# A four-layer transformer on one core: attention and output projection on pairs of fp16 instead of pairs of fp32r

## The reference

```python
q = _rmsnorm(x @ wq_a.T, q_a_ln_w) @ wq_b.T            # 32 heads x (64 nope + 64 rope)
ckv, k_pe = split(x @ wkv_a.T)                          # 64 + 64, shared by all heads
kv = _rmsnorm(ckv, kv_a_ln_w) @ wkv_b.T                 # per head: 64 of k_nope, 128 of v
q_pe, k_pe = rope(q_pe), rope(k_pe)
scores = (q_full @ k_full.T) * softmax_scale            # causal, 512 x 512 per head and batch
out = softmax(scores) @ v
x = x + out.reshape(B, S, 4096) @ wo.T
```

## Time and profile before

| what | us |
| --- | --- |
| device time, median of 3 runs | 1870.42 |
| the runs | 1863.43 to 1874.71 |
| the profiled execution, its own time | 1868.27 |
| its span | 1866.4 |
| `first` (to 172.0) | 172.0 |
| `lora_layer0` (to 441.0) | 269.0 |
| `projections` (to 533.7) | 92.7 |
| `attention` (to 1240.0) | 706.3 |
| `out_projection` (to 1602.0) | 362.0 |
| `lora_layer1` (to 1866.4) | 264.4 |

### The profile page before, as it was taken

The page is one execution under the profiler, slowest core; times in us unless marked ns, Lnnn a source line. Parts: engine busy times, 40 slices in busy tenths (PEclk is TensorE's granted clock), DMA queues, the critical chain, the costliest instruction groups (busy, mean ns, idle before and its releaser), DMA issues. The chain is left out here.

```text
span 1866.4 us, 32180 instructions
## 1 busy us (share of the span) xinstructions
PE 1716.2 (92%) x12720; PEld 1318.2 (71%) x12720; DVE 1045.2 (56%) x2405; ACT 889.3 (48%) x1600; POOL 753.7 (40%) x601
## 2 busy tenths in 40 slices
PE   6896699997789999999999999969999999589998
PEld 5564355554468888888888888857888888345654
DVE  6697465655766666666666666644324322244343
ACT  5553411103657877877877877843213111231110
POOL 3222244445647666675766675620000000134441
PEclk8798799998989999999999999979999999789999
DMA  9673423234418877978878877888445221332322
GB/s 328 215 250 123 130 57 91 68 91 107 87 35 141 164 160 142 165 145 162 148 161 143 162 150 145 151 205 277 136 137 190 91 96 63 103 85 68 91 68 79
DMA packets 514437, 252.39 MB, mean 135 GB/s; under 512 B 437104, under 2 KB 487280, under 8 KB 513904
## 3 DMA queue, kind: packets, MB, share of 16 engines
q1 hardware_dynamic: 514288, 250.34, 56.0%
HBM read 97.21 MB, written 44.04 MB: 76 GB/s over the span
## 5 line engine op out<-in xcount | busy, mean ns | idle before, releaser
L1568 POOL TENSOR_TENSOR xb<-xb 128x1280 f16<-128x1280 f32 x128 | 337.9, 2640 | 8.3 <-ACT xb L1462 8.3
L1505 DVE TENSOR_REDUCE D_sv<-D_S 128x1 f32<-128x512 f32 (+2 forms) x384 | 234.9, 640 | 114.9 <-PE D_S L1403 114.9
L48 PE MATMUL F_o<-F_wh,N_hT 128*128 128x384 f16 (+1 forms) x768 | 258.1, 336 | 6.5 <-DVE F_wl L780 6.5
L49 PE MATMUL F_o<-F_wl,N_hT 128*128 128x384 f16 (+1 forms) x768 | 257.9, 336 | 0.0
L50 PE MATMUL F_o<-F_wh,N_hT 128*128 128x384 f16 (+1 forms) x768 | 257.4, 335 | 0.0
L1454 ACT ACTIVATE xb<-D_S,D_sv 128x512 f32<-128x512 f32 (+3 forms) x512 | 241.8, 526 | 26.3 <-DVE D_sv L1505 26.1
L92 POOL TENSOR_SCALAR mv<-mv 128x1 f32<-128x1 f32 x64 | 27.2, 426 | 560.5 <-DVE mv L87 559.5
L48 PE MATMUL E_o<-E_mh,E_oh 128*128 128x512 f32 x512 | 200.5, 392 | 10.3 <-DVE E_ol L1734 10.3
L50 PE MATMUL E_o<-E_mh,E_ol 128*128 128x512 f32 x512 | 200.1, 391 | 0.0
L49 PE MATMUL E_o<-E_ml,E_oh 128*128 128x512 f32 x512 | 200.1, 391 | 0.0
L1574 POOL TENSOR_TENSOR D_qs<-D_qs,D_t 128x256 f32<-128x256 f32 x128 | 93.9, 734 | 234.5 <-DVE D_t L1531 234.5
(11 more groups left out here) (203 smaller groups left out, 3968.5 us busy)
## 6 DMA issues: line engine op xcount, KB each, us to landing
E_ro<-otd SPq DMA_DIRECT2D x58, 512.0 KB, 4.5
A_wo<-in_wo SPq DMA_DIRECT2D x16, 1024.0 KB, 6.0
otd<-h SPq DMA_DIRECT2D x64, 256.0 KB, 2.8
mwd<-A_mst SPq DMA_DIRECT2D x32, 256.0 KB, 2.4
xd<-xb SPq DMA_DIRECT2D x16, 512.0 KB, 3.5
E_rm<-mwd SPq DMA_DIRECT2D x16, 512.0 KB, 4.5
xb<-xd SPq DMA_DIRECT2D x16, 512.0 KB, 6.1
out_x<-xb SPq DMA_DIRECT2D x16, 512.0 KB, 3.1
```

Source lines behind the costliest of these rows:

```text
L48: e.matmul(out, a[0], b[0], start=start, stop=False, **kw)
L49: e.matmul(out, a[0], b[1], start=False, stop=False, **kw)
L1505: e.tensor_reduce(s[:, part:part + len(tiles)], Sb[n % 4][:, 0:N].rearrange("p (i k) -> p i k", i=len(tiles)), AX.X, ALU.min).then_inc(s_n ...
L1568: e.tensor_tensor(P2[u % 3][:, 1280:2560], P[u % 3][:, :], P2[u % 3][:, 0:1280], ALU.subtract).then_inc(s_pl, 1)
```

## The change

All that the latent attention and the output projection multiply is kept as fp16 pairs.

- **Scales.** The absorbed query weights are weighted with both norm vectors, given one scale for each head group, and split in the first adapter layer (`QueryWeights`, tiles 5 to 12 for the eight groups, results in `wbs`). Each group costs there two loads, four products on DVE (`dve_weigh`), a sum of squares (ACT), a matmul with ones (PE, a turn "s"), a scale (POOL), the inverse (DVE), the high part (ACT, 1024 elements for each partition) and the low part (DVE, the same), and a store. `wa`'s split moves from tile 6 to tile 3. The scale of M comes from sums of squares that ACT takes in `first` behind each evacuation of M (`msq`).
- **Projections.** No pointer scale at the split of q and k; POOL's `split_wb` is gone; group 0's weights are loaded ready.
- **Attention.** Scores use the exact tile widths (512, 384, 256, 128). The exponentials have the group's negative inverse scale as a pointer beside the bias, and the bias is the minimum times the inverse, which DVE computes in `bias(u, 0)` (behind `least(u, 1)`) and `bias(u, 1)` (behind `low_q(u+2)`). `least(u, 2)` is two reductions. PE's `turn_o` and ACT's `out_o` are replaced by `high_o` (ACT, 256 elements, every unit) and `low_o` (POOL, every unit); the outputs of four units are stored as an fp16 pair to `od`, not turned. Values and turned queries have a bank each.
- **Output projection.** M is split once, 1024 columns wide, with its scale; the split of the outputs is gone, since SP loads them with a transposing DMA into `OT` (three buffers; by quarters for the first three tiles, whole tiles of 32 blocks later). Both halves of a tile are computed in one pass; the sums are scaled back as they are added (two adds for a tile, pointer scale). M's first load waits for all stores of `attention`.
- **Second adapter layer.** The load of `mean` moves ahead of the last weight loads.

```diff
+    def dve_weigh(self, e, w, g, vec, lnr, wa):
+        u = self.u[g % 2]
...
+        for k in range(2):
+            un = u[:, k, 0:256].rearrange("p (h r) -> p h r", h=4)
+            e.scalar_tensor_tensor(un, un, vec[:, k:k + 1], lnr[:, :].unsqueeze(1).to_broadcast([128, 4, 64]), ALU.mult, ALU.mult)
+            i = e.tensor_scalar(u[:, k, 256:512], u[:, k, 256:512], vec[:, k:k + 1], wa.col(wa.INV), ALU.mult, ALU.mult)
+        i.then_inc(self.s_u, 1)
+    def act_square(self, e, w, g, junk):
+        w.wait_ge(self.s_u, g + 1)
+        e.activation(junk, self.u[g % 2], ACT.Square, accum_out=self.col(self.SQ, g)).then_inc(self.s_sq, 1)
+    def act_high(self, e, w, g):
...
+        e.activation(self.hl[g % 2][:, 0, :, :], self.u[g % 2], ACT.Copy, scale=self.col(self.SCALE, g)).then_inc(self.s_hi, 1)
+    def dve_low(self, e, w, g):
...
+        e.scalar_tensor_tensor(self.hl[g % 2][:, 1, :, :], self.u[g % 2], self.col(self.SCALE, g), self.hl[g % 2][:, 0, :, :],
+                               ALU.mult, ALU.subtract).then_inc(self.s_lo, 1)
...
# first, ACT
-                e.activation(mst[n % 4][:, :], mb[hf][:, :], ACT.Copy, scale=vec[:, 2:3]).then_inc(s_me, 1)
+                e.activation(mst[n % 4][:, :], mb[hf][:, :], ACT.Copy, scale=vec[:, 2:3]).then_inc(s_mc, 1)
+                e.activation(mb[hf][:, :], mb[hf][:, :], ACT.Square, scale=vec[:, 2:3],
+                             accum_out=msq[:, 2 * kt + hf:2 * kt + hf + 1]).then_inc(s_me, 1)
...
# lora_layer0
-    WA = 6
+    WA, QW, MS = 3, 5, 13
...
         if t == WA:
-            ORDER += [("s", 4)]
+            ORDER += [("s", 4), ("s", MS)]
+        if QW <= t < QW + 8:
+            ORDER += [("s", 5 + t - QW)]
...
# lora_layer0, DVE, loop over tiles
+            if QW <= t < QW + 8:
+                qw.dve_weigh(e, w, t - QW, vec, lnr, wa)
             gate(t)
             low_w(t)
+            if QW < t <= QW + 8:
+                qw.dve_inverses(e, w, t - QW - 1)
+                qw.dve_low(e, w, t - QW - 1)
             finish(t)
             adapter(t)
...
# attention
-                    M = max(128 * (i + 1), 256)
+                    M = 128 * (i + 1)
...
-                m = e.activation(p[:, AT[i]:AT[i] + N], Sb[n % 4][:, c:c + N], ACT.Exp, scale=-1.0, bias=s[:, 3 - i:4 - i])
+                m = e.activation(p[:, AT[i]:AT[i] + N], Sb[n % 4][:, c:c + N], ACT.Exp, scale=qw.col(qw.NEG, g), bias=s[:, 7 - i:8 - i])
...
+        def high_o(u):
+            g, b, h = units[u]
+            o = os[u // 4 % 2]
+            w.wait_ge(s_o, u + 1)
+            w.wait_ge(s_ot[u // 4 % 2], 16 * (u // 8))
+            e.activation(o[:, :, 0, 64 * h:64 * h + 64], on[u % 2][:, :, :], ACT.Copy).then_inc(s_oh, 1)
...
-            if pair(u - LAG - 1):
-                out_o(u - LAG - 1)
+            if there(u - LAG - 1):
+                high_o(u - LAG - 1)
...
+        def bias(u, n):
+            g, s = units[u][0], sv[u % 4]
+            w.wait_ge(s_neg, 3 * u + 2 + n)
+            e.tensor_scalar(s[:, 4 + 2 * n:6 + 2 * n], s[:, 2 * n:2 * n + 2], qw.col(qw.INV, g), None, ALU.mult).then_inc(s_bias, 1)
...
                 least(u, 0)
                 least(u, 1)
+                bias(u, 0)
...
             if there(u + 2):
                 low_q(u + 2)
+            if there(u):
+                bias(u, 1)
...
+        def low_o(u):
...
+            e.tensor_tensor(o[:, :, 1, 64 * h:64 * h + 64], on[u % 2][:, :, :], o[:, :, 0, 64 * h:64 * h + 64], ALU.subtract).then_inc(s_ol, 1)
...
# out_projection
+        for kt in range(16):
+            for j in range(G):
+                product(j, kt)
+        for j in range(G, NT):
+            for kt in range(16):
+                product(j, kt)
...
+                e.scalar_tensor_tensor(dst, ob[2 * (j % 3) + hf][:, :], ms.col(ms.INV), dst, ALU.mult, ALU.add).then_inc(s_add, 1)
...
+        for i in range(2):
+            w.wait_ge(s_ot[i], 16 * 16)
         load_m(0)
...
+        for j in range(G, NT):
+            w.wait_ge(s_col, j - 2)
+            e.dma_start_transpose(OT[j % 3][:, :, :, :, :].rearrange("p g l k c -> p (g l k) c"),
+                                  od[j, :, :, :, :].rearrange("p g l c -> p (g l c)")).then_inc(s_o[j % 3], 16)
...
# lora_layer1, SP
+        e.dma_start(mean[:, :], a["cst"][:, C_MEAN:C_N]).then_inc(lw.s_bias, 16)
```

More of the change, by code:

```diff
@@ new lines, with __init__, sem, col @@
+class FusedScale:
+    def __init__(self, nc, root, msq):
+        def sem(what):
+            return root.enter_context(nc.semaphore(f"ms_{what}"))
+        self.msq = msq
+        self.c = root.enter_context(nc.sbuf_tensor("ms_c", [128, 4], F))
+        self.s_sum, self.s_red, self.s_sc, self.s_inv = sem("sum"), sem("red"), sem("sc"), sem("inv")
+    def col(self, i):
+        return self.c[:, i:i + 1]
+    RAW, TOTAL, SCALE, INV = 0, 1, 2, 3
+    def pe_total(self, e, w, ones, bank):
+        e.matmul(bank[:, 0:32], ones[:, :], self.msq[:, :], start=True, stop=True).then_inc(self.s_sum, 1)
+    def dve_total(self, e, w, bank):
+        w.wait_ge(self.s_sum, 1)
+        e.tensor_reduce(self.col(self.RAW), bank[:, 0:32], AX.X, ALU.add).then_inc(self.s_red, 1)
+        w.wait_ge(self.s_red, 1)
+        return e.tensor_scalar(self.col(self.TOTAL), self.col(self.RAW), NORM2, 1e-30, ALU.mult, ALU.max)
+    def pool_scale(self, e, half):
+        e.tensor_tensor(self.col(self.SCALE), self.col(self.TOTAL), half, ALU.pow).then_inc(self.s_sc, 1)
+    def dve_inverse(self, e, w):
+        w.wait_ge(self.s_sc, 1)
+        e.reciprocal(self.col(self.INV), self.col(self.SCALE)).then_inc(self.s_inv, 1)
@@ L1079, in pool @@
                 scale(4)
+                scale(MS)
+            if QW <= t < QW + 8:
+                scale(5 + t - QW)
         norm.pool_rstd(e, w, N_F0 + NT + 3)
@@ L1421, in values @@
             m.then_inc(s_v, 1)
-        def turn_o(u):
-            ps, o = t_bank("o", u), os[u // 2 % 2]
-            w.wait_ge(s_o, u + 1)
-            bank_empty("o", u)
-            for i in range(4):
-                m = e.matmul(ps[:, 128 * i:128 * i + 128], o[:, i, :], ident, start=True, stop=True, is_transpose=True)
-            m.then_inc(s_to, 1)
         for u in range(FIRST, LAST):
@@ L1574, in add_q @@
             e.tensor_tensor(qv[:, :, 64:128], qv[:, :, 64:128], m[:, :, :], ALU.add).then_inc(s_qr, 1)
-        for u in range(FIRST, NU + 1):
+        def low_o(u):
+            g, b, h = units[u]
+            o = os[u // 4 % 2]
+            w.wait_ge(s_oh, u + 1)
+            e.tensor_tensor(o[:, :, 1, 64 * h:64 * h + 64], on[u % 2][:, :, :], o[:, :, 0, 64 * h:64 * h + 64], ALU.subtract).then_inc(s_ol, 1)
+        for u in range(FIRST, LAST):
             if there(u + AQ - 1):
-                g, b, tt = units[u + AQ - 1]
                 add_q(u + AQ - 1)
-                if g + 1 < 8 and b == 2 and tt in (0, 2):
-                    split_w(g + 1, tt // 2)
             if there(u - 1):
                 low_p(u - 1)
+            if there(u - LAG - 1):
+                low_o(u - LAG - 1)
     def sp(e):
@@ L1610, in sp @@
                 load_w(units[u + AQ][0] + 1)
-            if pair(u - LAG - 1):
-                store_o(u - LAG - 1)
+            if there(u - LAG - 2) and (u - LAG - 2) % 4 == 3:
+                store_o(u - LAG - 2)
     with nc.Block() as block:
@@ L1775, in dve @@
+        for kt in range(16):
+            low_m(kt)
+        for j in range(NT):
+            add(j)
+            if j == 3:
+                w.wait_ge(s_add, 2)
                 norm.dve_stats(e, w, N_F1, xb[:, 0, :])
```

471 lines of the change are left out of this document (197 added, 274 removed).

## The result

The changed kernel took 1891.59 us (median; 1889.33 to 1898.38), the kernel before 1866.93 us over all its runs beside it (1861.27 to 1874.71). The ratio is 1.0135 (95% interval 1.0086 to 1.0185): slower by 1.35%. The forecast was 1898 us. The profiled execution has a span of 1888.1 us, 21.7 more than before's.

What follows compares the result with a forecast made beforehand. PE was taken to bound the attention and output projection before, a closed ACT-DVE loop the attention after. Attention +17, projection -6, first adapter layer +16, first attention +2.5, rest -0.3 and +1: 1868.3 + 30 = 1898 us; range 1845 to 1930.

Steps and rivals of the forecast that it cites:

- The attention's sum: Latent attention: units of 5.47 us instead of 5.31, +17 us; +20.9 with the start of the output projection.
- the ACT loop: Latent attention: closed chain over ACT and DVE through exponentials, `high_q`, `low_q` and bias, forecast at 5.47 us per unit.
- The price of the exponentials' pointers: Latent attention: a scale pointer costs each exponential 0.09 us, making the pairs 1.34 and 0.91 us.
- the rival built on it: Latent attention: pointers and bias cost nothing in the loop, 5.1 us per unit, 1851 us in all; chance 0.14.
- So the turn is one closed loop, and its length is a sum: Latent attention: `exps(u,2)` waits for the bias, behind `low_q`, which waits for `high_q`; steps add to 5.42 us per unit.
- The rule of the Trainium skill: Latent attention: an SBUF-to-SBUF `tensor_scalar` can fully block against POOL; priced at some 0.05 us per unit, 6 us.
- The rival in which PE sets the pace: Latent attention: the loop does not close and PE's 4.6 us per unit decide, 1791 us in all; chance 0.07.
- The rival in which the bias waits for `low_o` as well: Latent attention: `bias(u,1)` also waits for POOL's `low_o`, +100 us, 1998 us in all; chance 0.08.
- Output projection: Faster fp16 matmuls -17 us, PE's wait for tile 3 4.9, slower matmuls after it 1.5; with startup and last add -6.
- Start of the output projection: M's load waits for the last store, so the first matmul comes 11.5 us after it, not 7.6: +3.9 us.
- First adapter layer: Splitting query weights delays a0 and turn "s": five tiles +1.5 us, two with `wa`'s split +3.3; +16 in all.
- First attention: 32 squares of M on ACT, 0.68 us each, nearly all in idle time: +2.5 us.

Runs made afterwards that it cites:

- e1: Changed kernel with a constant scale instead of the pointer in the exponentials, subtraction of the maximum left out: 1887.7 us, ratio 1.0115.
- e5: Changed kernel with both the constant exponential scale of e1 and the one-element bias instructions of e2: 1854.9 us, ratio 0.9951.
- e2: Changed kernel with each two-element bias instruction made two instructions of one element: 1897.2 us, ratio 1.0166.
- e3: Changed kernel with `bias(u,1)` ahead of `low_q(u+2)` instead of behind it: 1963.3 us, ratio 1.0521.
- e4: Changed kernel with `bias(u,1)` ahead of `low_q(u+2)` and each bias as two one-element instructions: 1799.7 us, ratio 0.9639.
- e8: e4 with the queries computed seven units ahead instead of six: 1768.9 us, ratio 0.9493.
- e6: Changed kernel with DVE's inverse and low part of the query weights behind the tile's own work in the first adapter layer: 1914.2 us, ratio 1.0278.
- e9: e6 with the weighing of the query weights also moved, behind the gates: 1891.5 us, ratio 1.0144.
- e11: Changed kernel with PE's turn "s" behind the next tile's first chunk, DVE's total and POOL's scale following it: 1889.0 us, ratio 1.0126.
- e7: Changed kernel with M's first load issued ahead of the wait for the stores and four buffers for turned outputs: 1885.1 us, ratio 1.0120.

## Why the prediction was right, and what in it was not

The time was right to 6 us (the forecast increase was 30 us, the span grew by 21.7) and the sign for a true reason: a chain through several engines, which fp16 does not shorten, closes at 5.45 us and not at PE's 4.5. Of its steps:

- **The attention's sum** came out at +21.8 for +20.9 by errors that cancel. The 127 periods are 16.2 us longer, for 17 with the short turns at the ends. From the last unit's first score matmul to the issue of the last store it is 24.1 us for 19.3 before, +4.7 that no term had, less 0.9 at the stage's start. In the last stretch the biases of the last two units took 2.54 us each beside `low_p`, and ACT idled 1.2 us for each (0.5 before); how much of the 4.7 us they make is not shown. The start of the projection is +1.8 for +3.9. None of the signs that the prediction named (the gap behind `high_q`, a unit over 5.2 us) could tell the two loops apart: all came, and the ACT loop did not set the pace.
- **The price of the exponentials' pointers** (0.09 each): right, 1.32 and 0.91 measured for 1.34 and 0.91, and 0.36 us in e1 for the four. But the rival built on it, 5.1 us without them, is refuted as a mechanism in this order: e1 took them away and the time stood still.
- **"So the turn is one closed loop, and its length is a sum"**: the loop is there (e5) and its length was right (the forecast's 5.42 without the meeting with POOL, 5.42 by e2, as an estimate). It does not set the pace. The step that failed is the next one, where POOL was put inside the loop with room to spare and its meeting with the bias was priced at "I take 0.05". The meeting is itself a loop: bias, two minima, `bias(u,0)`, rotate, `add_q`, `low_p`, bias, 5.446 us. It costs only some 0.03 us per unit over the ACT loop in after, so the period came out right by luck, the two loops being that close; but the waiting instruction is what any repair of ACT runs into: 0.36 us per unit in e1, 2.06 in the one instruction of e3.
- **The rule of the Trainium skill** (page "SBUF — State Buffer", section "Who interferes with whom", `tensor_scalar` from SBUF to SBUF fully blocks in its 2-port mode): I gave it 6 us. The traces agree with the rule for two elements: 0.27, 0.63 and 2.29 us, each ending 0.02 to 0.03 us after `low_p`. In e2 and e4 one element shows no such wait. To size it by the delay that it adds in one order was the mistake: it fixes when the instruction can end, and so closes a loop.
- **The rival in which PE sets the pace**, 1791 us, 0.07: rightly small for this code. e4 and e8 are that rival, once both loops are opened: 1800 and 1769 us.
- **The rival in which the bias waits for `low_o` as well**, 1998 us, 0.08: refuted for the steady state, where the bias comes while `low_p` still runs and is let in behind it, ahead of `low_o`. Three units near the end show the wait, 0.66 to 0.68 us in the bias.
- **Output projection**: fp16's gain as forecast. From first to last matmul it is 13.1 us shorter, where the terms gave 17 less 4.9 and 1.5. The wait for tile 3 was 4.25 us for 4.9. The terms are short by a wait of the kernel before, which is gone: the prediction has its matmuls "without a gap", but once PE waited 2.07 us for the split of the outputs.

```profile
1285.19 0.50 PE L48 MATMUL E_o<-E_mh,E_oh 128*128 128x512 f32 x1 [2.07 <-DVE E_ol L1734]
```

- **Start of the output projection**: 9.4 us from the last store's issue to the first matmul for 11.5: M's load was issued 2.5 us after the last store's issue ended, not 4.5 behind it, and was there in 3.9 us, not 4.5.
- **First adapter layer**: +12.4 for +16. The chain (high part, low part, `finish`, a0, "s") is the one forecast, 14.4 us for 14.7. The term that was too large is that of the tiles with `wa`'s split, 15.2 at most for 16.5. e6, e9 and e11 show that no single edit of that chain frees the tile: the load's buffer, POOL's add and the gates each come next. How much of the 1.2 us per tile could be hidden is left open.
- **First attention**: +0.5 for +2.5. The 32 squares take 0.66 us each and have 32 reads of the accumulator of 0.21 beside them that the forecast didn't count. No cost of them can be seen: from the first matmul of M (`A_m`) to the first chunk of the next stage it is 130.8 us before, 130.7 after, and 129.0 to 131.5 in the experiments, which all have this stage as in after. The stage's whole length differs more among them, 187.0 to 196.2 us, so neither +0.5 nor +2.5 can be told from nothing.

## What to carry to other kernels

When the bound engine gets faster, write down every closed chain through the others that a unit has to pass, not only the first one found; if two have nearly the same length, an experiment on one of them alone gains nothing, and only the edits together show what each is worth. An instruction that always ends with another engine's is waiting for it, however short its excess looks. And before moving an instruction into another engine's idle gap, look at what else runs in that gap.

## What the runs showed of the hardware

- A `tensor_scalar` of 128x2 fp32 from SBUF to SBUF, while POOL runs a `tensor_tensor` of 128x1280, takes what is left of POOL's instruction: up to 2.54 us in after and 2.30 in e3, instead of 0.23. It does the same beside POOL's 128x256 (`low_o`), 0.68 us. Two of 128x1 in its place take 0.20 each beside the same instructions, in all 512 of e2 and all 512 of e4 (0.22 at most). With the bias early, this alone is the difference between e3 and e4, 164 us.
- A `scalar_tensor_tensor` with two SBUF inputs of 128x256 took 2.23 us beside POOL's 128x1024 add (e9), and 0.48 without (after).
- A 512 KB load issued 0.8 us after a store of this size (e7) was ready for ACT 5.9 us later; issued 2.9 us after it (after), 3.9 us later.
